# Sparse attention in half-chunks on one core: three banks for the exponents instead of two, served as lanes of one key tile each, with the small products in the gaps of the third lane

## The chip, the cores and the metric

The program runs on 1 core of one Trainium2 chip. The metric is the device time of one execution in microseconds (us); lower is better. TensorE (PE) multiplies matrices, VectorE (DVE) and ScalarE (ACT) work elementwise, GpSimd (POOL) helps, SyncE (SP) issues transfers. Results of PE land in PSUM, which has eight banks of 128 x 512 words.

## The reference

Four stages act on x of shape (4, 512, 512): a sparse attention ("attention a"), a feed-forward, a second attention, and the feed-forward again. The change is inside attention a:

```python
pair = relu(h[:, :, None, :] - h[:, None, :, :] + b1)
sim = relu(pair @ W2.T + b2) @ W3.T + b3          # (B, 512, 512)
mask = -inf except at the 51 largest sim of each row
q, k, v = split(xn @ Wqkv.T + bqkv)               # 32 heads of 2 features
scores = q @ k.T / sqrt(2) + mask
ao = softmax(scores) @ v
x = x + y + ao @ Wout.T + bout                    # y = layernorm(x)
```

## The kernel before, in words

The stage "pairs" (the first third of the time) makes the mask. Then `attention_a` works through the 4 batch elements and 32 heads. 16 heads are a chunk `c` (8 chunks, two to a batch element), 8 heads a half-chunk `g` (16 of them). The steps are tuples in one list, written by `order_of_attention_a`; each engine's program takes its part of each step in the order of that list, so the list is the order on every engine, and an engine waits in place when a step isn't ready.

For a head `h` of half `g`:

- `scores g h pair i`: query tile by all 512 keys, on top of the mask (`mask` is multiplied in by the identity once for h = 0, and the heads' products are accumulated as differences on it). Two tiles (i = 0, 1) fill two banks, and VectorE takes both row maxima in one TENSOR_REDUCE. Pair 0 has banks 0 and 1, pair 1 has banks 2 and 3; a pair waits for the reduce of the one that had its banks last.
- `own_keys`: GpSimd makes the head's keys.
- `place g`: once the maxima of the half are there, PE turns them (side bank 7), ScalarE copies them to `max_t`, a transfer puts them under the queries in `qs`.
- `exp g keys h j`: the same product the other way round (keys by queries, tile `2 * keys + j`), now less the maximum, in bank 4 or 5 (j = 0, 1); ScalarE takes the exponential into `ex`, a ring of 24 tiles. Exp number i waits for the exponential of number i-2, which had its bank.
- `weighted c keys group j`: four heads' `ex` by their values, four matmuls side by side in the columns of the array, added up in bank 6 over the chunk.
- `turn` (turns a mask tile), and `divide`, `feature`, `project_a` (the end of a batch element) use bank 7 one after the other, one small step behind every second pair of exponents.

The last half-chunk (g = 15) is `last_exp`, two banks at a time in banks 0 to 3, woven with the first unit of the feed-forward.

One matter decides how matmuls of `scores` and `exp` lie beside each other. Both contract over 56 rows. The operands of an even half stand in partitions 0 to 55, of an odd half in partitions 64 to 119 (`own_keys(n, g % 2)`, `queries(g)`), so a matmul of an even half and one of an odd half use different row halves of the array.

The scores run ahead of the exponents by `LEAD` = 20 pairs; a half has 16 pairs. While half g's exponents are made, the scores are those of half g+1 for 12 of 16 steps (other row half) and of half g+2 for 4 of 16 (same row half).

Of the kernel before, what the change touches and what calls it, by code (L numbers as in the profile page):

```python
# [15 lines left out]
P = 128  # L16
# [57 lines left out]
def build(nc, d):  # L74
    with ExitStack() as ctx:
# [60 lines left out]
        x_added, ffn_stage = feed_forward(k, "ffn1", None, ffn_mem, Freed(a), a.var_made, a.sd_made)  # L136
# [59 lines left out]
LEAD, KEYS_AHEAD = 20, 1  # L196
# [43 lines left out]

def order_of_attention_a():
# [4 lines left out]
    side, weighted, places = [], [], []  # L246
    maxima = iter([(g, h, pair) for g in range(HALF_CHUNKS) for h in range(HEADS) for pair in range(2)])

    def next_maxima():
        at = next(maxima, None)  # L250
        if at is None:
            return [[], []]
        g, h, pair = at
        keys = HEADS * (g // 2) + h + KEYS_AHEAD
        if (h, pair) == (HEADS - 1, 1):
            places.append(("place", g))
# [3 lines left out]
    def place():  # L260

        while places and ("scores", places[0][1], HEADS - 1, 1, 1) not in order[-5:]:
            order.append(places.pop(0))

    for i in range(LEAD):
        for steps in next_maxima():
            order += steps
        place()
    for g in range(HALF_CHUNKS - 1):
        c, half = divmod(g, 2)  # L270
        b = c // 2
        if g % 4 == 0 and b + 1 < B:
            side += [("turn", b + 1, t) for t in range(NT)]
        for i in range(2 * HEADS):
            keys, h = divmod(i, HEADS)
            if weighted and h % 2 == 0:
                order.append(weighted.pop(0))
                if order[-1][1] % 2 and order[-1][2:] == (1, CHUNK // 4 - 1, 1):
                    side[:0] = finish_steps(order[-1][1] // 2)
            for j, scores in enumerate(next_maxima()):  # L280
                order += scores[:1] + [("exp", g, keys, h, j)] + scores[1:]
            place()
            if h % 4 == 3:
                weighted += [("weighted", c, keys, 2 * half + h // 4, j) for j in range(2)]
            if side and i % 2:
                order.append(side.pop(0))
            if (g % 4, i) == (1, 0) and b + 1 < B:
                order.append(("values", b + 1))
            if (g, i) == (HALF_CHUNKS - 4, 4):
                order.append(("early_root",))  # L290
    beside = iter(FIRST_ROWS)
    for h in range(HEADS):
        for keys in range(2):
            order.append(("last_exp", h, keys))
            if weighted:
                order.append(weighted.pop(0))
            order += next(beside, [])
        if h % 4 == 3:
            weighted += [("weighted", CHUNKS - 1, keys, 2 + h // 4, j) for keys in range(2) for j in range(2)]
    assert next(beside, None) is None  # L300
    order += [("operand", 0, 1), ("operand", 0, 2)] + weighted + side + [("product", 0, 11)]
# [4 lines left out]

OF_HEADS = ("own_keys", "values", "turn", "scores", "place", "exp", "last_exp", "weighted", "divide", "feature",
            "project_a", "early_root")


def finish_steps(b):
    steps = []
    for t in range(NT + 2):
        if t < NT:
            steps.append(("divide", b, t))
        if 1 <= t <= NT:
            steps.append(("feature", b, t - 1))
        if t >= 2:
            steps.append(("project_a", b, t - 2))
    return steps  # L320
# [33 lines left out]
class Freed:  # L354
# [3 lines left out]
    def __init__(self, a):  # L358
        self.a = a

    def rows(self, queue):
# [4 lines left out]
        queue.wait_ge(self.a.exp_in, 4 * HEADS * (HALF_CHUNKS - 2))  # L366

    def exp_banks(self, queue):

        queue.wait_ge(self.a.ex_made, 4 * HEADS * (HALF_CHUNKS - 1))  # L370

    def keys(self, queue):
        queue.wait_ge(self.a.exp_in, 4 * HEADS * (HALF_CHUNKS - 1) + 2 * HEADS)

    def last_banks(self, queue):

        queue.wait_ge(self.a.ex_made, 4 * HEADS * (HALF_CHUNKS - 1) + 2 * HEADS)
# [501 lines left out]
def attention_a(k, p, a, mem, nth):  # L879
# [6 lines left out]
    EXP_BANKS, OUT_BANK, SIDE_BANK = (4, 5), 6, 7  # L886
# [21 lines left out]
    side_bank, side_before, users, last = {}, {}, 0, {}  # L908
    for step in nth:
        if step[0] not in ("turn", "place", "divide", "feature", "project_a"):  # L910
            continue
        bank = SIDE_BANK
        if step[0] in ("divide", "feature", "project_a") and step[1] == B - 1:
            bank, users = (SIDE_BANK, EXP_BANKS[1])[users % 2], users + 1
        side_bank[step], side_before[step] = bank, last.get(bank)
        last[bank] = step

    def side_free(step):

        before = side_before[step]  # L920
        if before is None:
            if side_bank[step] != SIDE_BANK:
                pe.wait_ge(ex_made, LAST_EXP)
# [9 lines left out]
        else:  # L933
            pe.wait_ge(a.x_added, nth[before])

# [19 lines left out]
    LAST_EXP = 4 * HEADS * (HALF_CHUNKS - 1)  # L955

    def nth_exp(g, keys, h, j):
        return 2 * (HEADS * (2 * g + keys) + h) + j

# [6 lines left out]
    def nth_pair(h, keys):  # L966

        return LAST_EXP + 2 * h + keys

    def room(h, keys):  # L970

        i = (LAST_EXP + 4 * h + 2 * keys) % N_EX
        return ex[:, i:i + 2, :]

    def values_of(c, keys, h, j):
        g, own_h = 2 * c + h // HEADS, h % HEADS
        if g == HALF_CHUNKS - 1:
            return room(own_h, keys)[:, j, :]
# [1375 lines left out]
```

## Time and profile before

| | |
|---|---|
| median of 3 runs | 3208.04 us (3206.05 to 3209.53) |
| the profiled execution, its own time | 3192.71 us |
| its span | 3191.5 us |
| PE, DVE, ACT, POOL busy | 94%, 73%, 56%, 30% of the span |
| attention a: first scores to first exponents | 1068.2 to 1099.1 us |
| exponents of halves 0 to 14 | 1099.1 to 1564.3 us |
| last half and what follows it up to the first product of the feed-forward | 1564.3 to 1598.6 us |

A busy time that is near an engine's share of a stage doesn't say that the engine works at its peak there: PE's records overlap, so in this stage its waits are read from the starts of its matmuls.

### The profile page before, as it was taken

What the parts mean: (1) busy time and instruction counts of PE and PEld (TensorE: products, weight loads), DVE (VectorE), ACT (ScalarE), POOL (GpSimd) and SP (SyncE); (2) the same over time, 40 slices, a digit from 0 to 9 for tenths busy, and PEclk for the clock granted to TensorE, in tenths of its full rate; (3) what the DMA queues carried; (4) which work ended last, traced back from release to release, by engine and by line L of the source; (5) the groups of instructions that cost most, each with busy time, mean ns of one, the idle gap of its engine ahead of it and who ended that gap; (6) DMA issues with size and microseconds to landing.
All of it is one profiled execution on the core that took longest, in us unless ns stands there. A gap on an engine that the chain in (4) does not pass through costs nothing. (4 is left out here: it accounts for less than half of the span.)

```text
span 3191.5 us, 56935 instructions
## 1 busy us (share of the span) xinstructions
PE 3001.2 (94%) x22633; PEld 1755.6 (55%) x22665; DVE 2342.5 (73%) x4298; ACT 1779.0 (56%) x2921; POOL 960.3 (30%) x818
## 2 busy tenths in 40 slices
PE   6999999999999799999989999989999987999999
PEld 3545445445666333333368878864444434887787
DVE  6998999999999667666466676655766776667665
ACT  4988888888899365656643333323434443333332
POOL 1000000000000312211065655523544564565653
PEclk9999999999999699999999999999999998999999
DMA  2000000000000000000011111114323311112111
GB/s 74 2 2 12 2 2 12 2 2 12 2 2 2 1 1 1 1 1 1 21 47 50 50 47 53 50 67 122 99 79 87 100 34 46 50 50 76 50 52 48
DMA packets 106670, 112.95 MB, mean 35 GB/s; under 512 B 9827, under 2 KB 75364, under 8 KB 106021
## 3 DMA queue, kind: packets, MB, share of 16 engines
q1 hardware_dynamic: 103782, 108.61, 12.2%
q8 instruction: 181, 2.97, 0.4%
q10 hardware_dynamic: 2624, 0.69, 0.1%
q14 instruction: 83, 0.68, 0.1%
HBM read 84.76 MB, written 20.97 MB: 33 GB/s over the span
## 5 line engine op out<-in xcount | busy, mean ns | idle before, releaser
L746 DVE TENSOR_SCALAR pair_in<-key_words,row_words 128x512 f32<-128x512 f32 x1792 | 725.9, 481 | 33.8 <-PE ps L632 29.9
L831 ACT ACTIVATE pair_mid<-ps,row_bias 128x512 f32<-128x512 f32 x896 | 588.1, 690 | 115.6 <-PE ps L632 98.6
L632 PE MATMUL ps<-pair_in,w_hi 128*32 128x512 f16 x7168 | 626.6, 390 | 12.1 <-DVE pair_in L746 11.5
L1097 DVE TENSOR_REDUCE maxes<-ps 128x2 f32<-128x1024 f32 x256 | 306.5, 1223 | 154.1 <-PE ps L1011 153.0
L632 PE MATMUL ps<-pair_in,w_lo 128*32 128x512 f16 x3584 | 393.1, 389 | 0.0
L632 PEld LDWEIGHTS ps<-pair_in,w_hi 128*32 128x32 f16 x7168 | 257.1, 95 | 204.3 <-issue 35.1
L1141 ACT ACTIVATE ex<-ps 128x512 f32<-128x512 f32 x480 | 264.1, 595 | 179.9 <-PE ps L1031 169.1
L859 POOL TENSOR_SCALAR_AFFINE_SELECT sim<-sim 128x512 f32<-128x512 f32 x16 | 9.9, 616 | 1030.9 <-ACT sim L848 1030.9
L1507 PE MATMUL ps<-ffn_b_hi,ffn_a_hi 128*128 128x512 f32 x904 | 285.3, 397 | 23.9 <-DVE ffn_up L1595 9.2
L1507 PE MATMUL ps<-ffn_b_lo,ffn_a_hi 128*128 128x512 f32 x904 | 281.6, 393 | 2.3 <-DVE ffn_b_lo L1577 2.3
L1507 PE MATMUL ps<-ffn_b_hi,ffn_a_lo 128*128 128x512 f32 x904 | 280.4, 391 | 0.7 <-POOL ffn_a_lo L1738 0.7
L1645 DVE TENSOR_TENSOR x<-x,ps 128x512 f32<-128x512 f32 x256 | 175.5, 686 | 136.2 <-PE ps L1524 133.1
L647 PE MATMUL ps<-pair_mid,w_slide 128*32 128x512 f32 x2048 | 247.2, 592 | 0.0
L1031 PE MATMUL ps<-qs,own_keys 56*128 56x512 f32 x480 | 212.5, 466 | 32.9 <-ACT ex L1141 24.2
L2252 ACT ACTIVATE ex_b<-ps 128x512 f32<-128x512 f32 x256 | 147.4, 599 | 168.2 <-PE ps L2096 167.0
L2184 DVE TENSOR_REDUCE maxes_b<-ps 128x1 f32<-128x512 f32 x256 | 169.4, 682 | 86.7 <-PE ps L2081 86.2
L1011 PE MATMUL ps<-own_keys,qs 56*128 56x512 f32 x512 | 219.9, 478 | 1.9 <-DVE maxes L1097 1.2
L1507 PEld LDWEIGHTS ps<-ffn_b_hi,ffn_a_hi 128*128 128x128 f32 x904 | 168.8, 190 | 68.3 <-DVE ffn_up L1595 11.7
L1738 POOL TENSOR_TENSOR ffn_a_lo<-ffn_sums,ffn_a_hi 128x1024 fp32r<-128x1024 f32 x60 | 148.1, 2468 | 170.4 <-ACT ffn_a_hi L1660 170.4
L1507 PEld LDWEIGHTS ps<-ffn_b_lo,ffn_a_hi 128*128 128x128 f32 x904 | 171.1, 190 | 40.3 <-DVE ffn_b_lo L1577 4.3
L1705 ACT ACTIVATE ffn_gate<-ffn_gate 128x512 f32<-128x512 f32 x60 | 37.9, 632 | 275.4 <-DVE ffn_gate L1602 275.4
L1507 PEld LDWEIGHTS ps<-ffn_b_hi,ffn_a_lo 128*128 128x128 f32 x904 | 171.0, 189 | 37.3 <-POOL ffn_a_lo L1738 1.2
(233 smaller groups left out, 5269.1 us busy)
## 6 DMA issues: line engine op xcount, KB each, us to landing
ffn_raw_up<-in_w_ffn SPq DMA_DIRECT2D x64, 512.0 KB, 4.0
ffn_raw_down<-in_w_ffn SPq DMA_DIRECT2D x64, 256.0 KB, 2.7
q_stack<-halves SPq DMA_DIRECT2D x48, 256.0 KB, 5.1
k_stack<-halves SPq DMA_DIRECT2D x48, 256.0 KB, 5.9
halves<-hi_b SPq DMA_DIRECT2D x16, 512.0 KB, 2.7
halves<-lo_b SPq DMA_DIRECT2D x16, 512.0 KB, 3.6
out<-x SPq DMA_DIRECT2D x4, 1024.0 KB, 4.6
x<-in_x SPq DMA_DIRECT2D x6, 512.0 KB, 5.9
```

Source lines behind the costliest of these rows:

```text
L632: s = nc.tensor.matmul(ps[32 * quarter:32 * quarter + 32, bank + which, :], w_part[:, at_w:at_w + 32], words.rearrange("p (s two) -> p s t ...
L647: s = nc.tensor.matmul(ps[32 * c:32 * c + 32, 6 + w, :], p.w3_slide[:, 30 - 2 * r:62 - 2 * r], p.pair_mid[:, n % NG, half, :], start=r == ...
L746: s = nc.vector.tensor_scalar(p.pair_in[:, (4 * n + i) % N_PAIR, :], p.key_words[:, b % 2, :], p.row_words[:, b % 2, row:row + 1], None, A ...
L831: nc.scalar.activation(p.pair_mid[:, n % NG, which, :], ps[:, bank + which, :], ACT.Relu, bias=bias).then_inc(p.mid_made, 1)
L1011: s = nc.tensor.matmul(ps[:, t, :], queries(g)[:, t * P:t * P + P], own_keys(n, g % 2), start=False, stop=True, skip_group_check=True)
L1031: nc.tensor.matmul(ps[:, EXP_BANKS[j], :], own_keys(n, g % 2)[:, t * P:t * P + P], queries(g), start=False, stop=True, skip_group_check=Tr ...
L1097: nc.vector.tensor_reduce(maxes[:, g % 2, 2 * pair:2 * pair + 2, h], ps[:, 2 * pair:2 * pair + 2, :], AX.X, ALU.max).then_inc(maxes_made, 1)
L1141: nc.scalar.activation(ex[:, i % N_EX, :], ps[:, EXP_BANKS[j], :], ACT.Exp, scale=2.0 ** -0.5).then_inc(ex_made, 1)
L1507: i = nc.tensor.matmul(bank, a_part[:, s % 2, a_at, h, :], b_part[:, place(operand), h, :], start=opens and (which, m, h) == (0, 0, 0), st ...
L1645: nc.vector.tensor_tensor(x[:, n, :], x[:, n, :], ps[:, 6 + t % 2, :], ALU.add).then_inc(x_added, 1)
L1738: nc.gpsimd.tensor_tensor(lo, source, hi.bitcast(F32), ALU.subtract).then_inc(w_lo_made, 1)
L2184: nc.vector.tensor_reduce(maxes[:, n % 2, g, t:t + 1], ps[:, O1_BANKS[i % 3], :], AX.X, ALU.max).then_inc(max_made, 1)
```

## The change

The exponents get three banks, (4, 5, 7). Bank 7 is shared with the small steps. `exp g h t` is now named by half, head and key tile `t`. Three lanes, one to a bank, are filled with streams of one key tile of one half (8 heads each), and read row by row (lane 0, 1, 2): 25 rows, 75 places, for each chunk of 64 exponents and 11 small steps. The small steps stand in the lanes as well, mostly in lane 2. Lane 2 runs 4 rows ahead (`STAGGER`). Each of two halves of a chunk has exponents in flight at once. `scores` are spread evenly, 32 pairs over 75 places, and a `weighted` comes at least 4 places after the one before it and 3 after its exponents, at whatever point of a pair of scores that is. `LEAD` goes from 20 to 30 pairs, the last with four exponents beside them, and `place 0` comes four pairs ahead of the first exponents. The eight exponents of half 14, tile 3 move to among the `last_exp`. Waits are by the number of a step in the list.

```diff
-LEAD, KEYS_AHEAD = 20, 1
+LEAD, KEYS_AHEAD = 30, 1
+LANE_ROWS, STAGGER = 25, 4
...
+def lane_of(kind, *at):
+
+    if kind == "exp":
+        g, h, t = at
+        return 2 if (g, t) == (HALF_CHUNKS - 2, 3) else ((0, 1, 2, 0), (1, 2, 0, 1))[g % 2][t]
+    return {("project_a", 0): 0, ("turn", 2): 0, ("feature", 1): 1, ("turn", 0): 1}.get((kind, at[-1]), 2)
...
+    if c % 2 == 0:
+        return (heads(0, 0) + small("project_a", 0) + heads(0, 3) + heads(1, 2),
+                heads(0, 1) + heads(1, 0) + small("feature", 1) + heads(1, 3),
+                heads(0, 2) + small("divide", 0) + place(2 * c + 1) + small("divide", 1) + small("feature", 0)
+                + heads(1, 1) + small("divide", 2) + place(2 * c + 2) + small("project_a", 1) + small("divide", 3)
+                + small("feature", 2))
...
     for i in range(LEAD):
-        for steps in next_maxima():
-            order += steps
-        place()
-    for g in range(HALF_CHUNKS - 1):
...
+        first, second = next_maxima()
+        ahead = LEAD - 2 * STAGGER
+        beside = [("exp", 0, (i - ahead) // 2, 2)] if i >= ahead and (i - ahead) % 2 == 0 else []
+        order += first + beside + second + [("place", 0)] * (i == 2 * HEADS + 1)
+    lanes = [[step for c in range(CHUNKS) for step in lanes_of(c)[lane]] for lane in range(3)]
+    lanes[2][:STAGGER] = []
+    weighted, second, tick, last_burst = [(0, ("weighted", 0, 2, 0))], [], 0, 0
+    for row in range(LANE_ROWS * (CHUNKS - 1) + HEADS):
+        c, r = divmod(row, LANE_ROWS)
+        for lane in range(3):
+            step = lanes[lane][row]
+            order += second
+            second = []
+            if 2 * HEADS * 2 * (tick + 1) // (3 * LANE_ROWS) > 2 * HEADS * 2 * tick // (3 * LANE_ROWS):
+                first, second = next_maxima()
+                order += first
+            order += [step] if step else []
+            if weighted and weighted[0][0] <= tick and tick - last_burst >= 4:
+                order.append(weighted.pop(0)[1])
+                last_burst = tick
+            if step and step[0] == "exp" and step[2] % 4 == 3:
+                g, h, t = step[1:]
+                weighted.append((tick + 3, ("weighted", g // 2, t, 2 * (g % 2) + h // 4)))
+            tick += 1
...
         elif kind == "exp":
-            g, keys, h, j = at
-            b, n, t, i = g // 4, HEADS * (g // 2) + h, 2 * keys + j, nth_exp(*at)
+            g, h, t = at
+            b, n, bank = g // 4, HEADS * (g // 2) + h, bank_of[step]
             pe.wait_ge(in_place[g % 2], 16 * (g // 2 + 1))
-            pe.wait_ge(ex_made, i - 1)
+            bank_free(step)
```

**Where the order changes, first place: PE at the end of the lead.** L1011 is `scores`, L1031 `exp`, L1029 its mask, L1020 `place`, L998 `turn`, L1009 the mask of the scores. Before:

```order
L1011 MATMUL ps<-own_keys,qs 128x512 x4
L1020 MATMUL ps<-ident,maxes 8x128 x4
L1011 MATMUL ps<-own_keys,qs 128x512 x3
L1029 MATMUL ps<-mask_t,ident_bf 128x512
L1031 MATMUL ps<-qs,own_keys 128x512
L1011 MATMUL ps<-own_keys,qs 128x512
L1029 MATMUL ps<-mask_t,ident_bf 128x512
L1031 MATMUL ps<-qs,own_keys 128x512
```

In the changed kernel L1039 is `scores`, L1058 `exp`, L1057 its mask, L1048 `place`:

```order
L1039 MATMUL ps<-own_keys,qs 128x512 x2
L1048 MATMUL ps<-ident,maxes 8x128 x4
L1039 MATMUL ps<-own_keys,qs 128x512 x9
L1057 MATMUL ps<-mask_t,ident_bf 128x512
L1058 MATMUL ps<-qs,own_keys 128x512
L1039 MATMUL ps<-own_keys,qs 128x512 x4
L1058 MATMUL ps<-qs,own_keys 128x512
```

Nine matmuls of scores stand between `place 0` and the first exponent instead of three, and behind the first exponent four matmuls of scores before the next.

**Second place: PE in the middle of a chunk.** L1061 is `weighted` before; here are two of them with what is between:

```order
L1061 MATMUL ps<-ex,v_aug 12x512 x4
L1011 MATMUL ps<-own_keys,qs 128x512
L1031 MATMUL ps<-qs,own_keys 128x512
L1011 MATMUL ps<-own_keys,qs 128x512
L1031 MATMUL ps<-qs,own_keys 128x512
L1011 MATMUL ps<-own_keys,qs 128x512
L1031 MATMUL ps<-qs,own_keys 128x512
L1011 MATMUL ps<-own_keys,qs 128x512
L1031 MATMUL ps<-qs,own_keys 128x512
L1071 MATMUL ps<-ident,ao_t 128x128 x2
L1061 MATMUL ps<-ex,v_aug 12x512 x4
```

In the changed kernel L1085 is `weighted`, L1094 `divide`:

```order
L1085 MATMUL ps<-ex,v_aug 12x512 x4
L1058 MATMUL ps<-qs,own_keys 128x512
L1039 MATMUL ps<-own_keys,qs 128x512
L1094 MATMUL ps<-ident,ao_t 128x128 x2
L1039 MATMUL ps<-own_keys,qs 128x512
L1058 MATMUL ps<-qs,own_keys 128x512
L1039 MATMUL ps<-own_keys,qs 128x512
L1058 MATMUL ps<-qs,own_keys 128x512
L1085 MATMUL ps<-ex,v_aug 12x512 x4
L1039 MATMUL ps<-own_keys,qs 128x512
L1048 MATMUL ps<-ident,maxes 8x128 x4
```

A small step or a `weighted` now cuts the run of 56-row matmuls where it falls, between the two tiles of a pair of scores as well; before, each `weighted` stood behind whole pairs.

**Third place: PE in the last half.** L1045 is `last_exp` and L1461 turns tiles for the feed-forward. Before:

```order
L1061 MATMUL ps<-ex,v_aug 12x512 x4
L1045 MATMUL ps<-qs,own_keys 128x512 x2
L1461 MATMUL ps<-ident,ffn_z 128x128 x4
L1045 MATMUL ps<-qs,own_keys 128x512 x2
L1461 MATMUL ps<-ident,ffn_z 128x128 x4
```

In the changed kernel L1072 is `last_exp`, L1482 turns the tiles, and L1058 is an `exp` of half 14:

```order
L1085 MATMUL ps<-ex,v_aug 12x512 x4
L1072 MATMUL ps<-qs,own_keys 128x512 x2
L1058 MATMUL ps<-qs,own_keys 128x512
L1482 MATMUL ps<-ident,ffn_z 128x128 x4
L1072 MATMUL ps<-qs,own_keys 128x512 x2
L1482 MATMUL ps<-ident,ffn_z 128x128 x4
```

One more matmul stands beside every second `last_exp`.

## Rows read from the trace of the kernel before

**Rows 1.** The page: span, and groups of attention a.

```profile
span 3191.5 us, 56935 instructions
...
L1097 DVE TENSOR_REDUCE maxes<-ps 128x2 f32<-128x1024 f32 x256 | 306.5, 1223 | 154.1 <-PE ps L1011 153.0
...
L1141 ACT ACTIVATE ex<-ps 128x512 f32<-128x512 f32 x480 | 264.1, 595 | 179.9 <-PE ps L1031 169.1
```

**Rows 2.** Busy time by stretch of attention a, with granted clock.

```profile
core 0: us, PE busy (x) PEld busy (x) DVE busy (x) ACT busy (x) POOL busy (x), PEclk, DMA share, GB/s
1068.20:1099.10 30.90, 27.18 (x54) 11.42 (x54) 24.02 (x20) 1.87 (x2) 24.65 (x20) 0.50 0.00 1
1099.10:1161.50 62.40, 57.49 (x286) 21.84 (x290) 38.33 (x32) 38.14 (x70) 12.29 (x8) 0.92 0.00 1
...
1537.80:1564.30 26.50, 23.10 (x117) 7.81 (x118) 16.10 (x16) 17.85 (x33) 0.00 (x0) 1.00 0.02 4
1564.30:1576.20 11.90, 10.66 (x52) 4.51 (x52) 3.12 (x6) 10.14 (x14) 0.00 (x0) 1.00 0.43 128
1576.20:1589.90 13.70, 13.56 (x47) 5.19 (x48) 1.10 (x3) 4.43 (x6) 0.00 (x0) 0.50 0.00 0
...
1099.10:1564.30 465.20, 426.45 (x2149) 157.11 (x2178) 310.85 (x317) 284.25 (x528) 77.06 (x56) 0.99 0.01 1
```

**Rows 3.** Waits from 1099 to 1564.3 us: total, times, longest.

```profile
PEld ps L1031 <- ACT ex L1141: 98.3, 214, 1.5
...
PE ps L1061 <- ACT ex L1141: 7.3, 35, 0.3
```

**Rows 4.** Timeline, one round of the steady order, halves of different row halves: start, length.

```profile
1544.70 0.50 PE L1011 MATMUL ps<-own_keys,qs 56*128 56x512 f32 x1
...
1544.70 0.50 PE L1031 MATMUL ps<-qs,own_keys 56*128 56x512 f32 x1
...
1545.04 0.39 PE L1011 MATMUL ps<-own_keys,qs 56*128 56x512 f32 x1
1545.04 0.39 PE L1031 MATMUL ps<-qs,own_keys 56*128 56x512 f32 x1
...
1545.24 2.27 ACT L1141 ACTIVATE ex<-ps 128x512 f32<-128x512 f32 x4 [1.17 <-PE ps L1031]
...
1545.46 2.36 DVE L1097 TENSOR_REDUCE maxes<-ps 128x2 f32<-128x1024 f32 x2 [1.16 <-PE ps L1011]
...
1545.89 0.50 PE L1031 MATMUL ps<-qs,own_keys 56*128 56x512 f32 x1 [0.23 <-ACT ex L1141]
...
1546.80 1.05 PE L1061 MATMUL ps<-ex,v_aug 128*12 128x512 f32 x8
```

**Rows 5.** Timeline, scores and exponents of the same row half.

```profile
1340.69 0.38 PE L1031 MATMUL ps<-qs,own_keys 56*128 56x512 f32 x1
...
1341.00 1.05 PE L1061 MATMUL ps<-ex,v_aug 128*12 128x512 f32 x8
...
1341.98 0.50 PE L1011 MATMUL ps<-own_keys,qs 56*128 56x512 f32 x1
...
1342.32 0.39 PE L1031 MATMUL ps<-qs,own_keys 56*128 56x512 f32 x1
...
1342.55 0.39 PE L1011 MATMUL ps<-own_keys,qs 56*128 56x512 f32 x1
```

**Rows 6.** Timeline, a mask ahead of an exponent at full clock.

```profile
1286.32 0.39 PE L1029 MATMUL ps<-mask_t,ident_bf 128*128 128x512 bf16 x1
1286.64 0.18 PEld L1031 LDWEIGHTS ps<-qs,own_keys 56*128 56x128 f32 x1 [0.23 <-issue]
```

**Rows 7.** Timeline of the lead: reduces, and from `place 0` to the first exponent.

```profile
1074.09 8.83 DVE L1097 TENSOR_REDUCE maxes<-ps 128x2 f32<-128x1024 f32 x7 [0.18 <-PE ps L1011]
...
1094.65 1.01 PE L1020 MATMUL ps<-ident,maxes 128*8 128x128 f32 x4
...
1099.07 0.79 PE L1031 MATMUL ps<-qs,own_keys 56*128 56x512 f32 x1 [1.83 <-DMA qs<-max_t]
```

More of the change, by code:

```diff
@@ L269, in order_of_attention_a @@
-    for g in range(HALF_CHUNKS - 1):
[L270 to L290, printed above, removed]
+        first, second = next_maxima()
@@ L291, in order_of_attention_a @@
+    weighted = [step for _, step in weighted]
+    assert not second and next(maxima, None) is None
     beside = iter(FIRST_ROWS)
@@ L298, in order_of_attention_a @@
         if h % 4 == 3:
-            weighted += [("weighted", CHUNKS - 1, keys, 2 + h // 4, j) for keys in range(2) for j in range(2)]
+            weighted += [("weighted", CHUNKS - 1, 3, h // 4)]
+            weighted += [("weighted", CHUNKS - 1, t, 2 + h // 4) for t in range(NT)]
     assert next(beside, None) is None
-    order += [("operand", 0, 1), ("operand", 0, 2)] + weighted + side + [("product", 0, 11)]
+    order += [("operand", 0, 1), ("operand", 0, 2)] + weighted + [("product", 0, 11)]
     for among, steps in FIRST_UNIT:
@@ L304, in order_of_attention_a, with exponents_in @@
     return order + first_tail()
+def exponents_in(order):
+    steps = [step for step in order if step[0] in ("exp", "last_exp")]
+    return {step: i + 1 for i, step in enumerate(steps)}
 OF_HEADS = ("own_keys", "values", "turn", "scores", "place", "exp", "last_exp", "weighted", "divide", "feature",
             "project_a", "early_root")
[L311 to L320, printed above, removed]
 def attention_a_memory(k, mem):
@@ L354, with __init__ @@
 class Freed:
-    def __init__(self, a):
-        self.a = a
+    def __init__(self, a, order):
+        self.a, self.nth_exp = a, exponents_in(order)
+        self.rows_read = max(n for step, n in self.nth_exp.items() if step[0] == "exp" and step[1] < HALF_CHUNKS - 2)
+        self.lanes_read = max(n for step, n in self.nth_exp.items() if step[0] == "exp" and lane_of(*step) < 2)
     def rows(self, queue):
@@ L934, in side_free, with step_of @@
             pe.wait_ge(a.x_added, nth[before])
+    room, room_free, held = {}, {}, {}
+    first_weighted, last_weighted, at_room = {}, {}, 0
+    for step in nth:
+        if step[0] == "weighted":
+            first_weighted.setdefault(step[1], step)
+            last_weighted[step[1]] = step
+        if step not in nth_exp:
+            continue
+        tiles = 1 if step[0] == "exp" else 2
+        if at_room + tiles > N_EX:
+            at_room = 0
+        room[step], room_free[step] = at_room, 0
+        for j in range(tiles):
+            if step[0] == "exp":
+                g, h, t = step[1:]
+            else:
+                g, h, t = HALF_CHUNKS - 1, step[1], 2 * step[2] + j
+            room_free[step] = max(room_free[step], held.get(at_room + j, 0))
+            held[at_room + j] = nth["weighted", g // 2, t, 2 * (g % 2) + h // 4]
+        at_room = (at_room + tiles) % N_EX
+    def step_of(g, h, t):
+        return ("last_exp", h, t // 2) if g == HALF_CHUNKS - 1 else ("exp", g, h, t)
     dve.wait_ge(a.small, a.small_all)
@@ L1017, in tensor @@
             pe.wait_ge(maxes_made, 2 * HEADS * (g + 1))
-            side_free(step)
+            bank_free(step)
             for t in range(NT):
@@ L1083, in tensor @@
             pe.wait_ge(edges_made, EDGES)
-            side_free(step)
-            nc.tensor.matmul(ps[:, side_bank[step], :], ao_feat[:, t % 2, :], a.wout_t[:, :], start=True,
+            bank_free(step)
+            nc.tensor.matmul(ps[:, bank_of[step], :], ao_feat[:, t % 2, :], a.wout_t[:, :], start=True,
                              stop=True).then_inc(out_done, 1)
```

148 lines of the change are left out of this document (68 added, 80 removed).

## The prediction, made before the changed kernel ran

> **What bounds the kernel now.** I read the page first, then the stage by stretches, the list of waits, and the timeline of single rounds. The page [rows 1] says that neither VectorE nor ScalarE is the bound of attention a: the 256 reduces idle 154.1 us in wait for PE's scores, the 480 exponentials 169.1 us in wait for PE's products. Nothing else of the program is touched, so everything happens in the stretches of [rows 2]: a lead of 30.9 us (at the lower of PE's two clocks, granted 0.50), 465.2 us in which the exponents of halves 0 to 14 are made, and some 34 us of the last half, 13.7 of them at 0.50 again.
>
> In the 465.2 us PE is what the others wait for, but PE waits too: 214 times, 98.3 us, for ScalarE to give back one of the two exponent banks, and 7.3 us ahead of `weighted` [rows 3]. The round in [rows 4] shows how. Scores and exponent start together at 1544.70, the exponential starts at 1545.24, 0.54 later; the next product for that bank goes at 1545.89. Taking a bank round is 1.19 us. The four exponentials of the round last 2.27 us, then ScalarE idles while PE is in the `weighted` of 1546.80. So the loop over two banks and the block of 0.98 us (start of `weighted` to the next start, [rows 5]) add up; a third bank is the right medicine for that loop.
>
> **What PE has to do, before and after.** Starts of matmuls give PE's price list at full clock. Same row half: 0.23 us from start to start [rows 5]. Other row half: the two start together (1544.70 and 1544.70, 1545.04 and 1545.04, [rows 4]), so a pair of unlike halves costs one slot. Each run of 56-row matmuls between full-array steps costs 0.19 us extra: the second start comes 0.34 instead of 0.23 after the first, and the step behind it 0.31 instead of 0.23 after the last [rows 5]. `weighted` is 0.98 [rows 5], a mask ahead of an exponent 0.32 [rows 6].
>
> I counted the list from the first exponent of the main part to the first `last_exp`, for both kernels.
> - Before: 951 matmuls of scores and exponents in 621 slots, since 330 start with one of the other row half; 193 runs; 118 `weighted`; 60 exponent masks.
> - After: 920 matmuls in 769 slots, only about 151 start with another; 218 runs; 116 `weighted`; 58 masks.
>
> Why fewer share a slot: with a lead of 30 pairs spread evenly, the scores are mostly of the half with the same parity as the exponents beside them; only in the middle third of a chunk do two halves mix. The small products and the scores' masks are as many in both, and drop out. The difference is 148 x 0.23 + 25 x 0.19 - 2 x 0.98 - 2 x 0.32 = +36 us of work that PE didn't have. The price of alternation beyond three slots in a row isn't in the trace; I take 0.23 a slot there too. If every slot of an alternating run cost 0.34, the 151 shared ones would add 151 x 0.11 = 17 us.
>
> A rule of the Trainium skill speaks against the change here ("TensorEngine Tiling (Array Packing)", Key Properties: tiles work independently and in parallel, and a change of the tiling mode drains the engine; its table gives up to twice the speed for a contraction of 64 or less). By it alone, without the waits, the main part would be longer by the lost pairs and the added changes of mode. The trace agrees with both halves of it [rows 4, 5].
>
> **The waits.** To price them alike before and after, I compared for each product the PE work that the order puts between it and the last user of its bank (by the price list) with the loop that the bank needs: 1.19 us for an exponent [rows 4], and 0.42 + 1.23 + 0.05 = 1.70 us for a pair of scores (the last matmul at 1545.04 to the reduce at 1545.46, one reduce, the release, [rows 4]; the 1.223 mean is in [rows 1]). Before, 214 exponents come short, by 111 us in sum; the trace has 214 waits and 98.3 us, a ratio of 0.88, so the reckoning is good. After:
> - exponents: 96 come short, by 22.7 us in sum; x 0.88 = 20 us.
> - scores: 39 pairs come short, by 23 us (almost none before). They lie in the same middle thirds as the exponents' waits, and one wait relieves the other; I take half, 11.5 us. Bounds 0 and 23.
> - small steps in lane 2: next user 3 places (2 us) later, against some 2 us for `divide` and `project_a` to be read; 3 us in all.
> - reduces and exponentials that queue on VectorE or ScalarE when slots are dense, not shown before: the two rows nearest are a reduce's 1.14 spacing (2.36 for two, [rows 4]) and the third of the main part in which VectorE is idle [rows 2]. Between 0 and 30 us; I take 5, since the load stays below the span in every stretch.
>
> Sum 39.5 us. What goes away is 98.3 + 7.3 us, less 11 us of the former in which a scores matmul of the other row half waited along and so saved a slot of its own: 95 us. The low clock at the start of the main part (0.92 in its first stretch, [rows 2]) costs alike in both. Main part: +36 + 39.5 - 95 = -19.5 us, with -36 (only the exponents' 20 us are left) and +9 (all bounds of the waits taken high: 20 + 23 + 3 + 30 = 76, less what one wait relieves of another, 8) as its ends.
>
> **The lead.** Ten more pairs before the main part, at VectorE's pace of 1.26 us (8.83 us for 7, [rows 7]) = 12.6 us; the first exponent's mask in between about 1.2 more at the low clock. The stall of 1.83 us on the transfer of the maxima at 1099.07 goes, since `place 0` now has four pairs, 5 us, before the first exponent, against 4.42 from 1094.65 to 1099.07 [rows 7]. Together +12 us. These reduces are not made twice, but the main part was not bound by VectorE (310.85 of 465.2 us, [rows 2]), so doing them early earns nothing by itself; what it earns for PE is in the count (452 scores instead of 471 in the main part).
>
> **The last half.** Eight more exponents (0.34 each, one with a mask) and two more `weighted`: 8 x 0.34 + 0.32 + 2 x 0.98 = 5 us, of which some fall into the 1.2 us in which PE is idle in 1564.3 to 1576.2 [rows 2]: +4.5. PE was at 0.50 in 1576.2 to 1589.9, busy 13.56 of 13.7 us [rows 2], after a stretch in which it waited for bits of the feed-forward. With more work in that stretch the clock may stay up, which gives back up to half of 13.7, 6.8 us; I take half of that, 3.4. The last half: +1.
>
> **Sum.** -19.5 + 12 + 1 = -6.5 us, against the profiled execution's 3192.7 us: 3186. The median of the runs is 15 us above the profiled one; I see nothing in this stage that would make the difference, and take the same 6.5 off it: 3202.
>
> **The rivals.**
> - *The pipeline is nearly free of waits, and the clock holds.* For it: the round has four exponentials in 2.27 us and PE's share of a place (0.68 us in dense thirds: 1.85 slots and a fifth of a `weighted`) is above ScalarE's 0.5 and VectorE's 0.49. Then only 20 of the 39.5 us remain and the last half gets its whole 6.8 back: -6.5 - 19.5 - 3.4 = -29, some 3179. Against: the middle thirds, where a place costs 0.5 us on all three engines.
> - *Slower: scores cut in two.* 73 of 256 pairs of scores now have a `weighted` or a small step between their two tiles, none before. Each makes the reduce 1 us late, and VectorE, with only two pairs of banks, then hands them back late; PE stands in order with all lanes behind it. At 0.2 us lost for each beyond what is counted above, 73 x 0.2 = 15 us, the result is +8, just slower; at 0.3 us, 22 us, it is 3224. For it: the 39 short pairs. Against: in dense thirds a pair comes back 3.2 us later, and the loop even when cut is 1.70 + 1.2.
> - *It comes out even.* Lost sharing, lead and last half cost 36 + 12 + 1 = 49 us; if 46 us of waits stay instead of 39.5, within what the reckoning leaves open, the sum is 0 and the time 3208.
> - *Alternation costs 0.34 a slot*: +17, giving 3219, on the slower side too.
>
> **How the numbers follow.** The forecast (3202, its own range 3195 to 3207) 0.40, fewer waits (around 3179) 0.22, even (around 3208) 0.17, slower by cut pairs or alternation 0.21. Below 3201.6 (0.2% is 6.4 us, about what a measurement of this kernel can tell) lie the second case and six tenths of the first: 0.46. Above 3214.4 lies the slower side: 0.21. The rest is within, 0.33. The range leaves out the better part of the second case and the worse part of the slower ones, some 0.1 each: 3182 to 3219.
>
> **What would show it.** Right: the list of waits from the first exponents on has under 40 us for PE on ScalarE's exponentials (98.3 before), and new waits for the reduces of 10 us or so; the timeline in the outer thirds of a chunk has starts 0.23 apart and no waits; a chunk takes 60 to 62 us; the first main exponent is at about 1111 us, and the last half begins at about 1557. Wrong: waits for reduces of 40 us and more (cut pairs), starts 0.34 apart in the middle third (alternation), a chunk of under 58 us (fewer waits), or a clock of 0.50 far into the main part, which the longer lead with its idle PE could bring.

## The result and the profile after

The changed kernel takes 3240.68 us (median of 20 runs, 3209.01 to 3278.1), the kernel before 3206.3 us (20 runs, 3191.87 to 3215.01). The ratio is 1.0089, with a 95% interval of 1.007 to 1.0109: slower by 0.9%. The ratio leaves out the five longest runs of the changed kernel (3259.86 us and more), whose mean granted clock was lowest; the medians over all runs stand 1.011 apart. The forecast was 3202, range 3182 to 3219, with the sign the other way.

The profiled execution of the changed kernel took 3269.69 us, near the long end of its runs, at a mean granted clock of 0.937 where the median of the 20 runs is 0.950, so the low clock shown below is more than in a typical run. First the page: the span, and the groups that answer to those of [rows 1].

```profile
span 3268.4 us, 56967 instructions
...
L1120 DVE TENSOR_REDUCE maxes<-ps 128x2 f32<-128x1024 f32 x256 | 308.4, 1224 | 213.3 <-PE ps L1039 211.6
L1162 ACT ACTIVATE ex<-ps 128x512 f32<-128x512 f32 x480 | 263.1, 599 | 231.6 <-PE ps L1058 227.8
```

Both helpers idle more than before for PE: the reduces 212 us instead of 153, the exponentials 228 instead of 169. Their own times are the same. So PE's products come later. Next the busy time by stretch, which answers to [rows 2]; the columns are the same, and the seventh number, PEclk, is the one to read.

```profile
core 0: us, PE busy (x) PEld busy (x) DVE busy (x) ACT busy (x) POOL busy (x), PEclk, DMA share, GB/s
1068.80:1111.80 43.00, 39.59 (x78) 16.36 (x77) 35.05 (x30) 4.26 (x6) 24.71 (x20) 0.50 0.00 0
1111.80:1179.80 68.00, 67.96 (x203) 25.12 (x203) 27.73 (x23) 27.04 (x48) 1.56 (x1) 0.50 0.00 1
...
1193.90:1257.10 63.20, 61.61 (x297) 24.97 (x296) 38.79 (x33) 38.55 (x72) 12.71 (x9) 0.88 0.01 1
1389.00:1442.60 53.60, 51.74 (x254) 19.94 (x253) 36.81 (x46) 30.38 (x58) 7.14 (x9) 0.97 0.01 2
1442.60:1534.80 92.20, 92.16 (x277) 33.22 (x276) 38.31 (x35) 36.56 (x66) 8.76 (x6) 0.50 0.00 1
...
1111.80:1616.80 505.00, 494.81 (x2049) 191.49 (x2048) 292.95 (x296) 267.17 (x494) 77.20 (x56) 0.78 0.00 1
```

The lead ends at 1111.8 us, 12.7 us later than before. But then PE stays at 0.50 for another 68 us, though it is busy 67.96 of 68.0, and in 1442.6 to 1534.8 it falls back to 0.50 for 92 us in which it is never idle (92.16 of 92.20). Before, the clock rose 9.5 us after the first exponents and stayed up for the rest of the main part [rows 2]. The seven chunks from the first exponents on take 505.0 us at a mean of 0.78; before, the same seven took 438.7 us (1099.1 to 1537.8).

The waits of the same seven chunks, which answer to [rows 3]:

```profile
PEld ps L1039 <- DVE maxes L1120: 25.7, 44, 1.7
...
PEld ps L1058 <- ACT ex L1162: 16.2, 36, 1.2
...
PE ps L1058 <- ACT ex L1162: 1.6, 5, 0.8
```

The change does what it says: PE's waits for exponent banks are down from 98.3 us in 214 waits to 16.2 us in 36. The waits for the reduces need more care. The same row in the same seven chunks of the kernel before is no smaller:

```profile
PEld ps L1011 <- DVE maxes L1097: 32.7, 39, 0.9
```

But 38 of those 39 waits are weight loads that stood by while PE was in a `weighted` (0.85 us each, as the one at 1345.55), so PE itself lost nothing by them. In the changed kernel only 7 of the 44 are of that kind (7.7 us). New are the other 37, 18 us. Last, what a matmul costs where scores and exponents lie in the same row half: first a stretch of PE at full clock, then one at 0.50, both in the last third of a chunk (chunks 3 and 4).

```profile
1377.68 0.49 PE L1039 MATMUL ps<-own_keys,qs 56*128 56x512 f32 x1
1378.02 0.39 PE L1058 MATMUL ps<-qs,own_keys 56*128 56x512 f32 x1
1378.25 0.63 PE L1039 MATMUL ps<-own_keys,qs 56*128 56x512 f32 x2
1378.72 0.39 PE L1058 MATMUL ps<-qs,own_keys 56*128 56x512 f32 x1
1378.95 0.40 PE L1039 MATMUL ps<-own_keys,qs 56*128 56x512 f32 x1
...
1452.56 0.62 PE L1039 MATMUL ps<-own_keys,qs 56*128 56x512 f32 x1
1452.99 0.92 PE L1058 MATMUL ps<-qs,own_keys 56*128 56x512 f32 x2
...
1454.27 0.62 PE L1058 MATMUL ps<-qs,own_keys 56*128 56x512 f32 x1
1454.70 0.62 PE L1039 MATMUL ps<-own_keys,qs 56*128 56x512 f32 x1
```

At full clock the starts are 0.23 apart, as in [rows 5]; at 0.50 they are 0.43 apart. PE waits in neither. The page shows PE busy in both, so only the column of the granted clock tells them apart.

### The profile page after: what moved, and what is told of

It reads as the page before. It is cut to its first block and busy times, and to the rows that moved or that the text cites. A ratio compares the mean times of both kernels' runs of the same rounds, so it can differ in the third digit from the quotient of the medians.

```text
span 3268.4 us, 56967 instructions
## 1 busy us (share of the span) xinstructions
PE 3112.0 (95%) x22665; PEld 1792.2 (55%) x22665; DVE 2341.0 (72%) x4298; ACT 1780.4 (54%) x2921; POOL 960.8 (29%) x818
## 5 line engine op out<-in xcount | busy, mean ns | idle before, releaser
L1039 PE MATMUL ps<-own_keys,qs 56*128 56x512 f32 x512 | 259.5, 543 | 9.9 <-DVE maxes L1120 8.7
L1058 PE MATMUL ps<-qs,own_keys 56*128 56x512 f32 x480 | 220.9, 525 | 2.3 <-ACT ex L1162 2.1
L1202 POOL TENSOR_SCALAR own_keys<-ks,own_step 128x512 fp32r<-128x512 f32 x64 | 100.2, 1565 | 377.2 <-PE ps L1058 367.6
L1039 PEld LDWEIGHTS ps<-own_keys,qs 56*128 56x128 f32 x512 | 113.5, 236 | 177.5 <-issue 123.3
```

Of the source, the lines that this page charges most:

```text
L1039: s = nc.tensor.matmul(ps[:, t, :], queries(g)[:, t * P:t * P + P], own_keys(n, g % 2), start=False, stop=True, skip_group_check=True)
L1058: nc.tensor.matmul(ps[:, bank, :], own_keys(n, g % 2)[:, t * P:t * P + P], queries(g), start=False, stop=True, skip_group_check=True).then ...
```

## The experiments

Fourteen kernels can be compared: before, changed, and twelve variants of the two, each with one to three edits. In all of them the output is the whole computation. "Shared" is the count, from the list of steps, of matmuls of the main part that can start together with one in the other row half; "low" is the time at 0.50 between the first scores and 1600 us, in the profiled execution; it stops at 1600 us in every kernel, so it leaves out a part where attention a lasts longer (up to the last `last_exp` it is 276 us in the changed kernel, 483 in the kernel before with LEAD 30, 333 in that one with 64 rows, and 300 with the row half by chunk and LEAD 26). "Clock" is the mean granted clock of a whole execution, the median of all runs. Each variant's median stands beside one of the kernel before on the same chip in the same session: 3202.43, 3201.05 and 3206.43 us in the three sessions. The changed kernel itself was measured beside 3206.30, so a difference of two rows can hold some 5 us of difference between sessions; the ratios don't.

| kernel | shared | rows contracted | low, us | clock | time, us | ratio to before |
|---|---|---|---|---|---|---|
| before | 330 | 56 | 54 | 0.971 to 0.972 | 3206.30 | |
| changed | 151 | 56 | 251 | 0.950 | 3240.68 | 1.0089 (1.0070 to 1.0109) |
| before, LEAD 30 | 45 | 56 | 387 | 0.912 | 3388.17 | |
| before, LEAD 30, rows | 402 | 56 | 60 | 0.971 | 3200.56 | 1.0008 (0.9986 to 1.0029) |
| before, rows | 288 | 56 | 136 | 0.961 | 3224.09 | 1.0064 (1.0041 to 1.0088) |
| before, 64 rows | 330 | 64 | 59 | 0.975 | 3196.30 | 0.9965 (0.9952 to 0.9978) |
| before, LEAD 30, 64 rows | 45 | 64 | 240 | 0.944 | 3304.24 | |
| changed, whole pairs | 148 | 56 | 173 | 0.952 | 3230.90 | 1.0073 (1.0041 to 1.0106) |
| changed, rows | 319 | 56 | 158 | 0.958 | 3204.76 | 1.0005 (0.9983 to 1.0028) |
| changed, rows by chunk | 343 | 56 | 128 | 0.953 | 3215.57 | 1.0034 (1.0011 to 1.0058) |
| changed, rows by chunk, LEAD 26 | 273 | 56 | 233 | 0.946 | 3252.59 | 1.0137 (1.0106 to 1.0169) |
| changed, 64 rows | 151 | 64 | 87 | 0.970 | 3192.24 | 0.9977 (0.9957 to 0.9997) |
| changed, rows by chunk, 64 rows | 343 | 64 | 104 | 0.965 | 3184.69 | 0.9948 (0.9922 to 0.9973) |
| changed, rows, 64 rows | 319 | 64 | 100 | 0.968 | 3173.81 | 0.9893 (0.9878 to 0.9907) |

The two runs of LEAD 30 without the row edit have no ratio, since their runs are too few and too far apart (3328.93 to 3441.91, and 3224.18 to 3329.04); even their shortest are longer than any of before.

**Only the lead, in the kernel before.** The edit:

```diff
-LEAD, KEYS_AHEAD = 20, 1
+LEAD, KEYS_AHEAD = 30, 1
```

> The kernel before with LEAD = 30 and nothing else. Its scores then lie in the same row half as the exponents in 14 of 16 steps: 45 share a slot in the main part instead of 330; two exponent banks, whole pairs, small steps where they were. Theory 1: low clock far into the main part or in many stretches of it, as in the changed kernel, and 3260 or more. Theory 2 expects a low clock as well, from the longer lead, so this run alone doesn't part them; theory 3 (cut pairs, which this kernel doesn't have) expects a full clock and at most the 61 us of slots, less what hides in its waits: some 3230.

It took 3388.17 us, 186 us (5.8%) more than before in its session, with 387 us of low clock. No lanes, no cut pairs, no third bank is in it. Ten pairs more of lead turn the scores into the same row half as the exponents, in 14 of 16 steps. **The same with the row halves moved back:**

```diff
+def row_half(g):
+    return (g + g // 2) % 2
...
-                        to, at_g = 64 * half + 2 * HEADS * t, first + 2 * HEADS * g
+                        to, at_g = 64 * row_half(g) + 2 * HEADS * t, first + 2 * HEADS * g
...
-        return a.qs[64 * (g % 2):64 * (g % 2) + STACK, g // 4, g // 2 % 2, :]
+        return a.qs[64 * row_half(g):64 * row_half(g) + STACK, g // 4, g // 2 % 2, :]
...
-            s = nc.tensor.matmul(ps[:, t, :], queries(g)[:, t * P:t * P + P], own_keys(n, g % 2),
+            s = nc.tensor.matmul(ps[:, t, :], queries(g)[:, t * P:t * P + P], own_keys(n, row_half(g)),
```

The matmuls of `exp` and `last_exp` are edited in the same way.

> The kernel before with LEAD = 30 and the row half (g + g // 2) % 2: 402 share a slot. Lead and order are those of the run with LEAD = 30 alone. Theory 1: the clock is back at 1.00 soon after the lead, and the time is 3206 plus 12 for the lead less some 5: about 3213. Theory 2: the clock stays low as with LEAD = 30 alone, and the two runs differ by the slots only.

It took 3200.56 us. Order, lead, number and size of every instruction are those of the run above; only the partitions differ in which the operands stand, and 188 us are gone. The clock rises 7.0 us after the first exponents. These two runs settle most of the case: the longer lead as such doesn't hold the clock down. Most of the 188 us is the clock, not the lost sharing as such: at 1.00 throughout, a chunk takes 62.0 or 62.2 us with LEAD 30 and hardly any sharing (chunks 3 and 5 of the run with 64 rows below) and 58.2 or 58.5 with it (here), some 4 us a chunk. The busy time of the same two stretches, first without and then with the row edit:

```profile
1112.00:1212.00 100.00, 97.92 (x284) 41.61 (x288) 39.40 (x33) 41.36 (x70) 13.54 (x12) 0.50 0.00 1
1212.00:1296.00 84.00, 80.56 (x277) 32.97 (x281) 39.11 (x32) 38.28 (x67) 12.16 (x8) 0.66 0.00 1
```

```profile
1112.00:1212.00 100.00, 89.87 (x478) 31.47 (x482) 64.39 (x54) 64.00 (x117) 13.54 (x12) 0.97 0.01 1
1212.00:1296.00 84.00, 76.92 (x405) 27.13 (x407) 60.08 (x68) 51.23 (x97) 26.07 (x20) 1.00 0.00 1
```

In the first 100 us PE is busy 98 of 100 and gets 284 matmuls done at 0.50; with the other row half it is busy 90 and gets 478 done at 0.97. The PE whose neighbouring matmuls lie in the same row half was the busier one, and was granted half the clock.

**The row halves alone, in the kernel before** (the same edit as above, LEAD 20). It makes even halves share in all 16 steps and odd halves in 4.

> The kernel before, LEAD 20, with the row half (g + g // 2) % 2 and nothing else. Of its 951 matmuls 288 share a slot instead of 330, but unevenly: in even halves all 16 steps share, in odd halves 4 of 16. Theory 1: the clock falls in the odd halves and comes back in the even ones; low clock of 80 us and more in the main part (10 before), odd halves some 8 us longer, 3240 or more. Theory 2 (the clock has to do with the lead, or with lanes): full clock as before, and 42 slots more, 3206 to 3215.

3224.09 us, ratio 1.0064; 3240 or more was expected. The place is as expected. Chunk 2, its even half and then its odd half, and the chunk after it:

```profile
1218.10:1250.00 31.90, 29.65 (x158) 10.55 (x160) 23.18 (x32) 19.76 (x38) 7.30 (x8) 1.00 0.01 1
1250.00:1291.30 41.30, 40.34 (x156) 15.45 (x157) 23.82 (x25) 20.06 (x38) 12.48 (x8) 0.75 0.00 1
1291.30:1350.10 58.80, 53.97 (x279) 20.03 (x282) 38.49 (x32) 36.58 (x67) 6.30 (x5) 1.00 0.01 1
```

The half that shares runs at 1.00, the next, with as many matmuls, at a mean of 0.75 and 9.4 us longer (some 1.5 us longer in chunks 3 and 5, where both halves run at 1.00). But the chunk after it stays at 1.00 with its odd half unshared too, and so do two more of the seven: few shared matmuls make a fall likely, not certain. Chunks 2, 4 and 6, which fall, have a batch's last small steps in them, and in chunk 6 the even half fell too (0.50 for 44% of it); I didn't take that apart.

**Whole pairs, in the changed kernel.** A `weighted` no longer stands between the two tiles of a pair:

```diff
             order += [step] if step else []
+            order += second
+            second = []
             if weighted and weighted[0][0] <= tick and tick - last_burst >= 4:
```

> The changed kernel with both tiles of a pair of scores put ahead of a weighted step, so that no weighted step cuts a pair. Slots and row halves are as in the changed kernel (151 shared). Theory 3: 15 to 30 us faster than the changed kernel, 3210 to 3225, with fewer waits for reduces. Theories 1 and 2: within 10 us of the changed kernel's 3240, low clock for 150 us and more of attention a.

3230.90 us, ratio 1.0073. The edit leaves 29 of the 73 cut pairs cut, by a small step. In its seven chunks the row of waits for reduces is 14.0 us instead of 25.7, as theory 3 says, but the one for exponent banks is 52.5 instead of 16.2 (26 us of it while PE was in a `weighted`), and no gain clear of noise is left. So the cuts by `weighted` are not the cause of the loss. The 10 us between the medians may be the 78 us less of low clock or chance; the intervals of the ratios overlap. Low clock was 173 us, within what theory 1 named.

**The row halves, in the changed kernel** (the same edit as in the kernel before).

> The changed kernel with one edit: the row half of the array is (g + g // 2) % 2 instead of g % 2, so that the scores that run 30 pairs ahead lie in the other row half than the exponents beside them. By the count of the list 319 matmuls of the main part share a slot instead of 151. Theory 1 (unshared matmuls use half the rows, and the granted clock falls to 0.50 where most of them are unshared): the clock is 1.00 from about 1120 us on, the low clock inside attention a falls from 251 us to some 70, and the time is 3165 to 3190, faster than before. Theory 2 (the longer lead, in which PE idles, keeps the clock low whatever comes behind): the clock stays low far into the main part, and only the 39 us of slots come back at best: 3205 to 3230. Theory 3 (cut pairs of scores): little changes, over 3225.

3204.76 us, ratio 1.0005: the loss is gone, and 36 us come back from the placement alone, but it missed the 3165 to 3190. By its time alone it would fit theory 2 (3205 to 3230); against that theory stands the clock, which rises 6.8 us after the first exponents here too. Low clock is 158 us, not 70. Where PE falls, from the middle of chunk 1 on:

```profile
1185.00:1198.00 13.00, 12.31 (x72) 4.87 (x65) 8.67 (x9) 8.02 (x16) 0.00 (x0) 1.00 0.01 1
1198.10:1215.20 17.10, 16.77 (x54) 6.54 (x54) 7.32 (x7) 7.90 (x15) 0.00 (x0) 0.50 0.00 1
```

I count two matmuls as a pair that starts together if their starts in the trace are within 0.02 us. The outer thirds of a chunk, where some 15 pairs among 40 matmuls start together now (3 or 4 in the changed kernel), stay up nearly always. The middle thirds, in which this map leaves 7 pairs among 47 where the changed kernel had 10 or 11, spend half of their time low in five of seven chunks. So the low clock moved to where sharing is now least.

**The row half by chunk**, `g // 2 % 2`, for queries, keys and stacks, with the keys' ring grown from 16 to 21 tiles:

> The changed kernel with the row half given by the chunk, g // 2 % 2, so that all exponents of a chunk lie in one row half and the scores, nearly a chunk ahead, in the other, in every third of the chunk (the keys' ring grows from 16 to 21 tiles for it). 343 matmuls share a slot by count, against 151 in the changed kernel and 319 where the row half was (g + g // 2) % 2 but the middle thirds shared little. Theory 1 (the granted clock falls where few matmuls share a slot): no low clock in the middle thirds either, low clock inside attention a of 70 to 90 us, a chunk of 55 to 58 us, and 3165 to 3185. Theory 2' (the lanes as such, with their single steps and gaps, let the clock fall): low clock of 130 us or more remains, and 3195 to 3210.

3215.57 us, ratio 1.0034, a clear miss: 343 shared by count, the most of the lanes' variants, and yet not the fastest. The profiled execution, at 3192.76 us the shortest of the 12, has the middle thirds (18 pairs among 47 together) mostly up, and its low clock mostly in the first thirds (11 among 40). So the count of the whole list doesn't decide. In each of these maps the clock falls mostly where the least starts together, but no count parts the two levels: these first thirds fall with 11 where the last thirds, with 11 to 14, mostly stay up, and in the changed kernel the last third of chunk 3 and the first thirds of chunks 4 and 6 run at 1.00 throughout with 3 or 4. Nor is theory 2' ruled out as a part of the cause: 128 us of low clock in the best execution is next to the 130 that it named. **With LEAD 26** on top:

> As the run with the row half by chunk, and LEAD 26 instead of 30. The lead ends four pairs earlier, 5 us. Theory 1: 3160 to 3182, some 4 us below that run. If the stall on the transfer of the maxima comes back at the first exponents, only 3.

3252.59 us, ratio 1.0137, no faster than the changed kernel itself. The shorter lead takes the scores off the exponents' other row half at the start of a chunk (273 shared; 5 pairs together in a first third instead of 11), and 233 us are low. They lie where the sharing was lost: in six of the seven first thirds the clock is down for 22 to 30 us, while the middle thirds, untouched with 17 pairs, stay up but for 14 us in all. The 5 us of lead are lost many times over.

**More rows, nothing else, in the changed kernel.** The contraction takes 64 rows of each operand instead of 56. The eight added ones hold zeros, so nothing of the computation changes, and nothing shares that didn't.

```diff
-        return own[64 * half:64 * half + STACK, n % N_KEYS, :]
+        return own[64 * half:64 * half + 64, n % N_KEYS, :]
...
-        return a.qs[64 * (g % 2):64 * (g % 2) + STACK, g // 4, g // 2 % 2, :]
+        return a.qs[64 * (g % 2):64 * (g % 2) + 64, g // 4, g // 2 % 2, :]
```

> The changed kernel with 64 rows contracted instead of 56 in scores and exponents (the eight added rows hold zeros, so the result is the same). No matmul gets longer by it. If the clock is granted by how much of the array is in use, an eighth more rows could lift it a little: low clock in attention a below the changed kernel's 251 us by 30 us or more, 3215 to 3230. If it goes by other work (zeros switch nothing, or only the number of matmuls counts), nothing changes: 3235 to 3245.

3192.24 us, ratio 0.9977, with 87 us of low clock instead of 251. That is 48 us off the changed kernel's median (43 if each is taken against before in its own session), far more than expected, from multiplying zeros. Over all runs the granted clock is 0.970 instead of 0.950. Its first two chunks and the seven together:

```profile
1112.60:1169.30 56.70, 54.60 (x262) 22.27 (x264) 37.76 (x32) 35.27 (x66) 11.69 (x8) 0.94 0.01 1
1169.30:1226.60 57.30, 54.88 (x293) 22.64 (x296) 38.31 (x33) 38.08 (x72) 12.54 (x9) 1.00 0.01 2
1112.60:1542.80 430.20, 411.11 (x2022) 165.47 (x2048) 290.24 (x296) 262.74 (x494) 77.20 (x56) 0.96 0.01 1
```

The seven chunks take 430.2 us at 0.96, against 505.0 at 0.78 in the changed kernel and 438.7 before. The matmuls are no shorter: at full clock a last third of a chunk takes 17.5 us in both, and the longer first thirds 20.0 and 21.0 us in the changed kernel, 20.0 to 21.3 here. Only the share of the time at full clock differs. **The controls, in the kernel before:**

> The kernel before with 64 rows. It has nearly no low clock in its main part, so the added rows can give nothing there, if they work by the clock alone: 3196 to 3206, same as before. If 64 rows make matmuls themselves cheaper in some way, it is faster by 5 us or more here too.

> The kernel before with LEAD 30 (45 shared, 387 us of low clock in attention a, 3388 us) with 64 rows. Use decides: a large part of the low clock goes, some 3260 to 3330. Use doesn't decide, and the 48 us by which 64 rows lowered the changed kernel came from elsewhere: over 3370.

Where the clock was up anyway, 64 rows give 3196.30, ratio 0.9965, that is 0.35% (11 us); its main part in the profiled execution is not shorter (chunks of 59.7 and 65.4 us, as before). The gain goes with the clock all the same: over its four runs it is 0.975, against 0.971 for before in that session, and before's own runs lose 17 us for each 0.01 of clock, which makes some 7 of them. The two profiled executions, both at 0.975, differ by 0.9 us (3193.61 and 3192.71). In which stage the clock is better isn't recorded. With LEAD 30, 64 rows take 84 us off the median, 3304.24 instead of 3388.17 (four runs each, which just touch), and 147 us off the low clock. The effect is uneven: chunks 3 to 5 are at 1.00 now, chunks 0 and 1 are as low as without it (0.50 and 0.66), and chunk 6 is lower (0.57 instead of 0.71).

**Both, in the changed kernel.** Row half (g + g // 2) % 2 and 64 rows, and the row half by chunk and 64 rows:

> The changed kernel with both edits: row half (g + g // 2) % 2 (319 shared) and 64 rows contracted instead of 56. If the clock goes by how much of the array is in use, sharing and rows add up: low clock in attention a of 60 to 90 us (158 with the row half alone, 87 with 64 rows alone), chunks of 55 to 57 us since the slots are fewer, 3165 to 3185, faster than before. If the lanes' middle thirds have a floor of their own, as the 158 us suggest, 3185 to 3200.

> The changed kernel with the row half by chunk (343 shared) and 64 rows. Same reasoning: 3160 to 3185 if use of the array decides the clock; over 3195 if the low clock in its first thirds (128 us in attention a with 56 rows) comes from something else than use.

3173.81 us (four runs), ratio 0.9893, and 3184.69 us, ratio 0.9948. Both times are in the expected ranges, the second barely, but the low clock of the first, 100 us, is above the expected 60 to 90. It is 1.1% faster than before and the fastest of all. Its seven chunks:

```profile
1110.70:1523.50 412.80, 388.24 (x2022) 143.08 (x2048) 289.65 (x296) 261.45 (x494) 77.20 (x56) 0.95 0.01 1
```

412.8 us, 26 us less than before. That is what three lanes are worth when most of the clock and of the shared slots is kept. It isn't a better clock that does it, since over all runs the granted clock is 0.968, against 0.971 before. What the sharing is worth by itself can be read from chunk 3 of the two kernels with 64 rows, both at 1.00, first without and then with the row edit:

```profile
1290.10:1350.10 60.00, 57.55 (x299) 23.27 (x301) 41.33 (x39) 38.20 (x73) 12.51 (x9) 1.00 0.01 1
```

```profile
1283.80:1340.70 56.90, 54.01 (x299) 20.09 (x301) 41.18 (x39) 38.08 (x73) 12.50 (x9) 1.00 0.01 1
```

It is 3.1 us a chunk, 22 us in seven.

## Why the prediction was wrong

- **The lead, +12 us: right.** First main exponents at 1111.8 us, forecast about 1111.
- **The waits for exponent banks, 98.3 us to 20: right.** 16.2 us in 36 waits in seven chunks, plus 5.4 us ahead of the masks there. A slow PE waits less, but that isn't why: with 64 rows and the clock at 0.96 they are 19.5 and 7.6. The reckoning by distance in the list against the loop of 1.19 us held for a kernel that it hadn't seen.
- **The waits for reduces, 11.5 us with bounds of 0 and 23: low, but within the bounds.** 18 us of waits that were not there before, of 25.7 in the row. Uncutting 44 of the 73 pairs gave no gain that can be told from chance, so nothing bears out the price that the rival of the cut pairs needed.
- **The work of PE, +36 us of slots at the full clock's prices: the price at full clock was right, the premise that these prices hold was wrong.** Starts of the same row half are 0.23 us apart at 1.00, and the thirds of a chunk that ran at full clock throughout take 20.0 and 21.0 us (first), 20.9 and 21.8 (middle) and 17.5 (last), some 59 us a chunk (forecast 60 to 62; before, the mean was 62.7). At 0.50 they are 0.43 apart. The prediction costed the lost sharing as slots only. As slots it was even priced high: the 168 shared matmuls that the row edit gives back are worth 22 us at full clock, where 168 x 0.23 makes 39; with them PE waits more for the exponent banks (27.5 us in the seven chunks instead of 19.5, both with 64 rows).
- **The step that failed** is the sentence that the low clock at the start of the main part "costs alike in both". The term for it was nothing. The clock was low for 9.5 us there before and for 68 us after; it fell again for 92 us, and for some 60 us more in shorter falls. Seven chunks at full clock would take some 415 us, and they took 505.0, so about 90 us of the profiled execution are this step. Its whole main part, 1111.8 to 1636.8, took 525.0 us instead of 465.2: +60, where -19.5 was forecast. What bears on the clock was in the prediction's own count, 330 shared matmuls against 151. Shown by experiment: moving operands to the other row half, with the order untouched, moved the low clock up to 1600 us from 387 to 60 us and the time from 3388 to 3201, and eight rows of zeros moved it from 251 to 87 us and the time from 3241 to 3192. That the clock goes by how much of the array is in use fits both, but is argued: no run here tells use apart from something else that changes with placement and row count.
- **The last half, +1 us with half of the old low stretch given back: about right.** From the first `last_exp` to the first product of the feed-forward it takes 36.7 us (1636.8 to 1673.5) instead of 33.7 (1564.9 to 1598.6), +3 us. The clock is low for 10.2 us of it instead of 13.7, so only a quarter of the low stretch was given back.
- A slip that changed nothing: with only the exponents' 20 us left, the main part's low end is 36 + 20 - 95 = -39, not -36.
- The forecast did name "a clock of 0.50 far into the main part" among what would make it wrong, but blamed the longer lead with its idle PE for it and gave it no chance of its own. The lead isn't it: with the row halves moved back, the same lead ends 12.6 us later than before, and the clock rises 7 us after its end. The prediction drew on the Trainium skill ("TensorEngine Tiling (Array Packing)", Key Properties: tiles work in parallel, and a change of the tiling mode drains the engine) for the speed of the matmuls alone. The trace agrees with that, with two starts at 1544.70 [rows 4] and 0.34 instead of 0.23 us to the second start of a run [rows 5]. The placement also moved the clock, and that had no term.

At an equal clock the change is a gain. Over the 20 runs the changed kernel's time falls by some 25 us for each 0.01 of mean granted clock (a straight line through all of them), from 3278.1 us at 0.937 to 3209.0 at 0.961. Drawn out to the 0.975 of the profiled execution before (3192.71), that makes some 3180. This is argued from a slope that is drawn beyond the runs. The kernel with both edits shows it with fewer slots as well: 3173.81 us at a clock no higher than before's.

What stays open: why some chunks with the same steps fall and others don't, in one execution; why the map by chunk falls in its first thirds; what the rows of zeros change that the clock goes by; and in which stage the kernel before with 64 rows has its better clock.

## What to carry to other kernels

When PE's work is rearranged, count two things from the order: how many matmuls can start together in different rows of the array, and where the stretch with the fewest of them lies. Then ask what the granted clock does there; a PE that is busy 100% at 0.50 looks the same in its busy time as one at 1.00. Where short contractions leave rows unused, try filling them with zeros (here 64 rows instead of 56), and a placement of operands by which neighbours in the order lie in different row halves, before any change of the order is judged.

## What the runs showed of the hardware

- PE that is never idle can be at the lower clock of 1.2 GHz: busy 92.16 of 92.20 us at 0.50, with most neighbouring matmuls in the same row half. In the kernel with LEAD 30 it was busy 98 of 100 us at 0.50 at the start of the main part.
- The same instructions in the same order, with operands in other partitions, ran 188 us (5.5%) faster.
- Rows of zeros in the contraction bear on the clock: 64 instead of 56 rows took 164 us of low clock out of attention a in the profiled executions, raised the median clock from 0.950 to 0.970, and made no matmul longer. In the kernel before with LEAD 30 they did it in some chunks and not in others.
- Matmuls of alternating row halves cost one slot for two, in longer runs as well: in the changed kernel with the row edit pairs start at 1230.32, 1230.66 and 1230.89. With most sharing the chunks of the lanes take 56.6 to 56.9 us where their clock is full.
- With a fluctuating clock a kernel's own runs spread more: 3209 to 3278 us in the changed kernel, 3192 to 3215 before, 3170 to 3177 in the best one (four runs only).
